# Decoder layer: key roundings moved between engines, the last cross values of a head put ahead, and the cross values of two key blocks made together

## The chip, the cores and the metric

One core of a Trainium2 chip runs the whole kernel. The metric is device time in microseconds (us), lower is better. Three timed executions of the kernel before took 523.75 to 525.77, median 524.22.

## The reference

A decoder layer on `x` (1024 queries, width 128, 16 heads of width 8), everything in fp32:

```
x = layernorm(x + self_attention(x))              # one shared key/value head, 1024 keys
x = layernorm(x + cross_attention(x, ctx, mask))  # 6404 keys, 16 heads, masked keys get -1e9
x = layernorm(x + expert(x))                      # router, top 1 of 8 experts, weight = its probability
```

`self_attention` and `cross_attention` are softmax(Q K^T / sqrt(8)) V with projections and biases. The mask kills a range of keys; with the data here two groups of 640 keys are live.

## The kernel before

**Layout.** Scores are computed twice. As *rows* (queries on partitions, keys along the free axis, into PSUM tiles `RT[0]`, `RT[1]`) they only give the maximum per query, which VectorE (DVE) reduces at L883. As *columns* (keys on partitions, 512 queries along the free axis, into `ST[0..2]`) with the maximum already subtracted they go through ScalarE's exponential (ACT, L1065) into `prob`, and TensorE (PE) multiplies `prob` by the values into `O` (L1199, the function `add_values`). A head's maxima are needed before its columns, so rows run one head ahead of the columns.

**Cross attention.** `T` counts a pair (640 keys, five blocks of 128) of a head. There are 16 heads and n = 2 pairs, 32 `T` in all. PE's order is written out by hand. `other_blocks` does blocks b = 1 to 4: the column product of query half 0 (k = 2b), a row product of unit b-1, the column product of half 1 (k = 2b+1), a row product, and then the values of block b-1. `next_blocks` does block 0 of the next `T`, row units 4 and 5 (short ones of 128 keys), and the values of block 4. `clear_o` zeroes `O` for a new head, once `copy_o` on ACT has emptied it. A column product and a row product use different halves of the array's rows (`STACK`) and run side by side; the values use 128 rows and four groups of 32 columns.

**What orders it.** Column product k writes bank `BANK[k]` and waits until the exponential that last used the bank is done: `AGAIN[k]` is how many products back that was.

```python
BANK = (2, 0, 1, 2, 0, 1, 0, 2, 0, 1)
AGAIN = tuple(min(d for d in range(1, NCOL) if BANK[k - d] == BANK[k]) for k in range(NCOL))
```

So products 6 and 8 have a distance of 2, 7 and 9 a distance of 4, the others 3. The values of block b wait for the exponentials of both of its halves. GpSimd (POOL) rounds the keys from `Kl` into `Kr` and `Kc`, copies values to `vst`, and splits the maxima; SyncE's (SP) queue loads keys and carries the maxima (`max_rows`).

**Between self and cross attention.** The last self head's sums (`den`) and outputs (`aTr`) come back by DMA, DVE takes the reciprocal (`sums_back`), PE spreads it and projects (`project_out`), the layernorm follows, PE transposes `x` and makes the first cross queries. The keys of the second pair are rounded by DVE (`keys_of_pair`). The same `project_out` follows cross attention, and then the router and the experts (L1516, L1523 on PE, L930 on DVE).

`warm_up(o, count)` is `count` throw-away products of 512 columns into a free bank.

Of the kernel before, what the change touches and what calls it, by code (L numbers as in the profile page):

```python
# [5 lines left out]
F32 = mybir.dt.float32  # L6
# [10 lines left out]
P = 128  # L17
# [24 lines left out]
RU = 6  # L42
# [17 lines left out]
def decoder_layer(nc, t, out):  # L60
    ctx = ExitStack()
    with ctx:
# [9 lines left out]
        def dram(name, shape, dt=F32):  # L72
# [117 lines left out]
            "in_xT in_w0 in_r in_w in_bo cst0 cst q_clean pen_rows bias_ready bias_moved parts_known "  # L190
            "w0_ready warm sel_made bq_scaled s_k_ready s_k_hi s_k_z s_k_stack s_v_ready bias_copied vs_made "
# [46 lines left out]
        def _(sp):  # L238
# [35 lines left out]
            def o_rows(a, g):  # L274
# [5 lines left out]
                load(den[g * DH:(g + 1) * DH, :], osb[DH:P:32, g % 2, :], a + "_o_back")  # L280
# [4 lines left out]
            def o_back(a):  # L285
# [5 lines left out]
                load(den[0:h * DH, :], od[a][0:h, :, DH, :], a + "_o_back")  # L291
# [119 lines left out]
        def _(pool):  # L411
# [40 lines left out]

            low_q("s")
# [39 lines left out]
            p0 = pool.snap(pool.value_load(steer[0:1, 0:1], min_val=0, max_val=NP - MIN_PAIRS))  # L493

# [117 lines left out]
        def _(dve):  # L612
# [71 lines left out]
            def stack_k(h):  # L684
                w = slice(h * HALF, (h + 1) * HALF)
                dve.wait_ge(S("s_k_hi"), h + 1)
                v.tensor_scalar(kz[:, w], ST[1 + h][:, :], rowk[:, 1:2], kcon[:, 0:1], ALU.mult, ALU.add) \
                    .then_inc(S("s_k_z"), 1)
                dve.wait_ge(S("s_k_z"), h + 1)
                v.scalar_tensor_tensor(out=Kself[:, w], in0=khi[:, w].bitcast(F32), scalar=rowk[:, 6:7], in1=kz[:, w],  # L690
                                       op0=ALU.mult, op1=ALU.add).then_inc(S("s_k_stack"), 1)

            stack_q0("s", 0)
            stack_k(0)
            dve.wait_ge(S("in_r"), 48)
            v.tensor_scalar(bq["s"][:, :], bq["s"][:, :], SCALE, None, ALU.mult).then_inc(S("bq_scaled"), 1)
# [25 lines left out]
            for r in range(HEADS * SELF_U):  # L722
# [6 lines left out]
                if r == 0:  # L729
                    stack_k(1)  # L730
                if r == 2:
                    stack_q0("s", 1)
# [52 lines left out]
            def keys_of_pair(c, i):  # L785

                dve.wait_ge(S("x_k_ready"), i + 1)
                if c and not isinstance(i, int):
                    dve.wait_ge(S("kd_out"), i * 64)
                v.tensor_scalar(kx_f[c][:, :], RT[1][:, 0:PAIR], bk_x[:, 0:1], None, ALU.add).then_inc(S("x_k_f"), 1)  # L790
                v.tensor_scalar(kx_hi[c][:, :], RT[1][:, 0:PAIR], bk_x[:, 0:1], None, ALU.add).then_inc(S("x_k_hi"), 1)
                dve.wait_ge(S("x_k_f"), i + 1)
                dve.wait_ge(S("x_k_hi"), i + 1)
                v.tensor_tensor(kx_lo[c][:, :], kx_f[c][:, :], kx_hi[c][:, :].bitcast(F32), ALU.subtract) \
                    .then_inc(S("x_k_lo"), 1)


            keys_of_pair(0, 0)
# [145 lines left out]
        def _(act):  # L944
# [69 lines left out]
            act.wait_ge(S("bq_scaled"), 1)  # L1014
# [25 lines left out]
            with act.Fori(0, n1) as i:  # L1040
                act.wait_ge(S("x_v_ready"), act.snap(i + 2))
# [539 lines left out]
```

## Time and profile before

| | |
|---|---|
| median of three timed executions | 524.22 us |
| the profiled execution | 524.29 us, its span 522.6 us |
| busy share of the span | PE 93%, DVE 82%, ACT 69%, POOL 37% |
| start to first self columns | 0 to 32.7 us |
| self attention | 32.7 to 203.4 us |
| between the attentions | 203.4 to 247.0 us |
| cross attention, first columns to last values | 247.0 to 472.8 us |
| project, router, experts, layernorm | 472.8 to 522.6 us |

The span is the time from the first to the last instruction of one profiled execution; 1.7 us lie outside it. A busy PE is not an array at its peak: products overlap and waits for the array's draining count as busy.

### The profile page before, as it was taken

The numbers are of one execution on the slowest core, as the hardware profiler recorded it, in microseconds if no ns is written. First come the engines' busy times: TensorE is split into PE (matmuls) and PEld (weight loads), VectorE is DVE, ScalarE is ACT, GpSimd is POOL, SyncE is SP. The second block draws the span as 40 slices with busy tenths as digits, with TensorE's granted clock in tenths as the row PEclk, the third lists the DMA queues.
The fourth block names the chain that finished last, engine by engine and source line by source line (L and its number), as shares of the span: only waits on it lengthen the run. The fifth ranks groups of instructions, "written<-read, shape, count | busy, mean of one in ns | idle before, by whom it ended". The sixth has DMA issues, their size and how long they took to land.

```text
span 522.6 us, 13768 instructions
## 1 busy us (share of the span) xinstructions
PE 486.1 (93%) x4122; PEld 199.5 (38%) x4122; DVE 430.0 (82%) x639; ACT 358.7 (69%) x682; POOL 192.3 (37%) x300
## 2 busy tenths in 40 slices
PE   7989999999999998578999999999999999998793
PEld 2423333333333344423344444444444444435441
DVE  4999999999999825759889899899999998704478
ACT  6238888888888864330778878788888888882220
POOL 3214889889890000032233333233333323210010
PEclk9999999999999999989899999999999999999698
DMA  3389997877300014423233111111111111011001
GB/s 93 100 261 325 278 327 284 306 285 291 144 13 12 12 54 132 149 62 99 48 69 79 40 38 38 40 32 34 38 36 32 35 36 32 25 56 44 1 0 43
DMA packets 21770, 52.56 MB, mean 101 GB/s; under 512 B 5021, under 2 KB 13375, under 8 KB 19649
## 3 DMA queue, kind: packets, MB, share of 16 engines
q1 hardware_dynamic: 18461, 22.46, 16.4%
q0 software_dynamic: 2304, 28.84, 14.7%
q8 instruction: 37, 0.61, 0.5%
q10 hardware_dynamic: 932, 0.37, 0.3%
q14 instruction: 36, 0.29, 0.2%
HBM read 42.10 MB, written 8.94 MB: 98 GB/s over the span
## 4 chain that ended last, share of the span: by engine, by line
PE 76%; DVE 12%; ACT 5%; issue 3%; DMA 2%; ACTq 0%; SPq 0%; DVEq 0%
PE O L1199 30%; PE ST L1425 14%; PE RT L1397 9%; PE ST L1230 9%; PE RT L1216 4%; DVE mxs L726 3%; ACT prob L1028 2%; DVE x L930 2%; PE RT L1523 2%; DMA Qs<-mxr 2%; DVE mxc L883 1%; ACT osb L989 1%; PE O L1170 1%; PE RT L1120 1%; PE O L1195 1%
## 5 line engine op out<-in xcount | busy, mean ns | idle before, releaser
L883 DVE TENSOR_REDUCE mxc<-RT 128x1024 f32 (+1 forms) x192 | 196.8, 1046 | 24.0 <-PE RT L1397 19.5
L1065 ACT ACTIVATE prob<-ST 128x512 f32<-128x512 f32 x320 | 175.2, 595 | 44.4 <-PE ST L1425 44.1
L1028 ACT ACTIVATE prob<-ST 128x512 f32<-128x512 f32 x256 | 138.6, 597 | 26.5 <-PE ST L1230 15.9
L726 DVE TENSOR_REDUCE mxs<-RT 128x2 f32<-128x1024 f32 x128 | 152.9, 1224 | 3.2 <-PE RT L1216 1.0
L1397 PE MATMUL RT<-Kr,Qs 64*128 64x128 f32 (+1 forms) x512 | 119.5, 373 | 3.7 <-ACT big L975 2.2
L1425 PE MATMUL ST<-Qs,Kc 64*128 64x512 f32 x320 | 121.3, 453 | 1.2 <-DMA Qs<-mxr 0.7
L1199 PE MATMUL O<-prob,vst 128*9 128x256 f32 x1280 | 99.7, 383 | 0.6 <-ACT prob L1065 0.6
L1216 PE MATMUL RT<-Kself,Qs 64*128 64x512 f32 x256 | 89.2, 450 | 3.2 <-DVE Kself L690 1.4
L1230 PE MATMUL ST<-Qs,Kself 64*128 64x512 f32 x256 | 91.2, 450 | 0.4 <-DMA Qs<-mxr 0.4
L1199 PE MATMUL O<-prob,Vs 128*9 128x256 f32 x1024 | 79.3, 381 | 1.5 <-ACT prob L1028 0.7
L1425 PEld LDWEIGHTS ST<-Qs,Kc 64*128 64x128 f32 x320 | 54.0, 186 | 52.5 <-ACT prob L1065 26.7
L1397 PEld LDWEIGHTS RT<-Kr,Qs 64*128 64x128 f32 x512 | 58.8, 185 | 31.0 <-DVE mxc L883 26.0
L509 POOL CAST Kr<-big 128x512 fp32r (+1 forms) x64 | 29.1, 456 | 94.0 <-DMA big<-pd 71.8
L465 POOL TENSOR_SCALAR big<-big 128x3520 uint8<-128x3520 uint32 x16 | 49.9, 3117 | 23.2 <-DMA big<-in_mask 23.1
L1230 PEld LDWEIGHTS ST<-Qs,Kself 64*128 64x128 f32 x256 | 37.4, 184 | 50.7 <-ACT prob L1028 37.5
L534 POOL COPY vst<-Vx 128x27 f32 x64 | 13.1, 205 | 106.7 <-PE O L1199 105.8
L1216 PEld LDWEIGHTS RT<-Kself,Qs 64*128 64x128 f32 x256 | 35.7, 184 | 11.5 <-DVE mxs L726 6.0
L1199 PEld LDWEIGHTS O<-prob,vst 128*9 128x9 f32 x1280 | 19.0, 88 | 51.3 <-ACT prob L1065 35.4
L509 POOL CAST Kc<-big 128x256 fp32r (+1 forms) x64 | 29.2, 456 | 24.9 <-PE ST L1425 24.7
L1199 PEld LDWEIGHTS O<-prob,Vs 128*9 128x9 f32 x1024 | 15.2, 88 | 45.1 <-ACT prob L1028 38.2
L469 POOL TENSOR_TENSOR big<-big 128x880 int32<-128x880 int32 x14 | 29.1, 2081 | 1.2
L949 ACT ACTIVATE rstd<-mv,eps 128x4 f32<-128x4 f32 x6 | 1.8, 297 | 27.5 <-DVE mv L815 27.5
(220 smaller groups left out, 349.2 us busy)
## 6 DMA issues: line engine op xcount, KB each, us to landing
big<-in_mask POOLq DMA_DIRECT2D x16, 1760.0 KB, 7.6
big<-kd SPq DMA_DIRECT2D x66, 80.0 KB
od_s<-osb SPq DMA_DIRECT2D x14, 128.0 KB, 3.1
od_x<-osb SPq DMA_DIRECT2D x14, 128.0 KB, 1.8
Qs<-qd_s SPq DMA_DIRECT2D x12, 128.0 KB, 6.9
Qs<-qd_x SPq DMA_DIRECT2D x12, 128.0 KB, 3.8
qd_s<-Vx SPq DMA_DIRECT2D x2, 512.0 KB, 4.0
qd_x<-big SPq DMA_DIRECT2D x2, 512.0 KB, 4.5
```

The lines of the kernel that those rows point to most:

```text
L465: g_.tensor_scalar(sums if q == 0 else dead8, maskI[m % 2].bitcast(U32), 1.0, 0.0, ALU.min, ALU.max) \
L469: g_.tensor_tensor(sums.bitcast(I32), sums.bitcast(I32), dead8.bitcast(I32), ALU.add) \
L509: g_.tensor_copy(dst, Kl[:, ds(slot, 1), k0:k1].rearrange("p o k -> p (o k)")).then_inc(S(name), 1)
L726: v.tensor_reduce(mxs[:, h % 2, c2, :].rearrange("p (f t) -> p f t", f=2)[:, :, q], RT[r % 2][:, :].rearrange("p (f k) -> p f k", f=2), AX ...
L883: v.tensor_reduce(o, src, AX.X, ALU.max).then_inc(S("x_row_free"), 1)
L1028: nc.scalar.activation(prob[:, c % SLOTS, k * HALF:(k + 1) * HALF], ST[(2 * c + k) % 3][:, :], ACT.Exp) \
L1065: nc.scalar.activation(prob[:, b, (k % 2) * HALF:(k % 2 + 1) * HALF], ST[BANK[k]][:, :], ACT.Exp) \
L1199: mm = mmul(O[32 * q:32 * q + VW, 0:256], v, prob[:, slot, q * 256:(q + 1) * 256], start=False, stop=False, skip_group_check=True)
L1216: mm = mmul(RT[r % 2][:, f * HALF:(f + 1) * HALF], Qs[STACK[f], h, q * P:(q + 1) * P], Kself[STACK[f], c2 * 512:(c2 + 1) * 512], start=Tru ...
L1230: mmul(ST[(2 * c + f) % 3][:, :], Kself[STACK[f], b * P:(b + 1) * P], Qs[STACK[f], g, :], start=True, stop=True).then_inc(S("s_col_ready"), 1)
L1397: mm = mmul(o, Qs[STACK[f], h, q * P:(q + 1) * P], Kr[STACK[f], w], start=True, stop=not gen, skip_group_check=True)
L1425: mm = mmul(o[:, :], Kc[STACK[f], b, :], Qs[STACK[f], g, :], start=True, stop=not gen, skip_group_check=True)
```

## The change

Key and query roundings at the start: the sign and sum of the second half of the self keys and of the second self head move from DVE (`stack_k(1)`, `stack_q0("s", 1)`) to POOL as two operations each, and the part `kz` of that half to ACT. The second pair's cross keys move from DVE to ACT (two roundings) and POOL (the difference). The wait for `den` is separated from the wait for `aTr`. In cross attention, `other_blocks` makes the values of blocks 0 and 1 together after block 2's scores and those of 2 and 3 together after block 4's; at a head change `next_blocks` makes row unit 4 and the last values ahead of the new head's column products. ACT copies `O` before the new head's first exponential. The first cross rows start before the other queries are projected. `warm_up` counts change from 16 to 14 and from 8 to 18 (after the output projection, in both attentions). The expert biases' eight products are split into two groups of four. `BANK` is unchanged.

```diff
-                load(den[g * DH:(g + 1) * DH, :], osb[DH:P:32, g % 2, :], a + "_o_back")
+                load(den[g * DH:(g + 1) * DH, :], osb[DH:P:32, g % 2, :], "den_in")
...
+            def stack(o, hi, z, sign, name):
+                g_.tensor_scalar(hi, hi.bitcast(F32), sign, None, ALU.mult).then_inc(S("stack_signed"), 1)
+                pool.wait_ge(S("stack_signed"), 1 if name == "s_k_stack" else 2)
+                g_.tensor_tensor(o, hi.bitcast(F32), z, ALU.add).then_inc(S(name), 1)
...
+            stack(Kself[:, HALF:Q], khi[:, HALF:Q], kz[:, HALF:Q], rowk[:, 6:7], "s_k_stack")
...
+            stack(Qs[:, 1, :], q0hi["s"][1], q0z["s"][1], rowk[:, 7:8], "s_q0_stack")
             low_q("s")
...
+            with pool.Fori(0, n1) as i:
+                wait_count(pool, S("x_k_f"), i + 2)
+                wait_count(pool, S("x_k_hi"), i + 2)
+                wait_count(pool, S("kd_out"), i * 64 + 64)
+                g_.tensor_tensor(kx_lo[1][:, :], kx_f[1][:, :], kx_hi[1][:, :].bitcast(F32), ALU.subtract) \
+                    .then_inc(S("x_k_lo"), 1)
...
-                if r == 0:
-                    stack_k(1)
-                if r == 2:
-                    stack_q0("s", 1)
...
             def sums_back(a):
-                dve.wait_ge(S(a + "_o_back"), 16 * 15)
+                dve.wait_ge(S("den_in"), 48 * ("sx".index(a) + 1))
                 v.reciprocal(rden[:, :], den[:, :]).then_inc(S(a + "_rden"), 1)
 
             def project_out(a):
+                dve.wait_ge(S(a + "_o_back"), 16 * 12)
...
-            dve.wait_ge(S("s_pv"), HEADS * SELF_U)
-            with dve.Fori(0, n1) as i:
-                keys_of_pair(1, dve.snap(i + 1))
...
+            nc.scalar.activation(kz[:, HALF:Q], ST[2][:, :], ACT.Identity, bias=kcon[:, 0:1], scale=rowk[:, 1:2]) \
+                .then_inc(S("s_k_z"), 1)
...
+                act.wait_ge(S("kd_out"), act.snap(i * 64 + 64))
+                nc.scalar.activation(kx_f[1][:, :], RT[1][:, 0:PAIR], ACT.Identity, bias=bk_x[:, 0:1]).then_inc(S("x_k_f"), 1)
+                nc.scalar.activation(kx_hi[1][:, :], RT[1][:, 0:PAIR], ACT.Identity, bias=bk_x[:, 0:1]).then_inc(S("x_k_hi"), 1)
...
             for g in range(HEADS):
                 T0 = act.snap(n * g)
-                step_exp(T0, 0)
                 if g:
                     copy_o("x", g - 1, act.snap(T0 * NBLK + NBLK))
+                step_exp(T0, 0)
                 step_exp(T0, 1)
...
-                    warm_up(ST[2], 16)
+                    warm_up(ST[2], 14)
...
-                warm_up(ST[2], 8)
+                warm_up(ST[2], 18)
...
-                        if turn:
+                        if b == 4 and h_turn is not None and h_turn < HEADS:
                             pe.wait_ge(S("x_mx_copied"), h_turn + 1)
-                        values(g, T, b - 1, e + 2 * b)
+
+                        if b % 2 == 0:
+                            values(g, T, b - 2, e + 2 * b)
+                            values(g, T, b - 1, e + 2 * b)
...
+                    if g != g_before and not first:
+
+                        if h < HEADS:
+                            rows(1, 4, h, U)
+                            rows(0, 4, h, U)
+                        values(g_before, T_before, NBLK - 1, e + NCOL)
+                        have_max("x", g)
+                        for f in range(2):
+                            col(g, T, f, e + (NCOL + 1 + f - AGAIN[f]))
+                            if h < HEADS:
+                                for q in (2, 3):
+                                    rows(1 - f, 5, h, U, [q])
+                        return
...
+                have_queries("x", 0)
+                if not gen:
+                    rows_alone(0, 0, range(2))
+                for h in range(2):
+                    project_q("x", wq_x, h, 1 + h)
+                rows_alone(0, 0, range(0 if gen else 2, RU))
+                with pe.Fori(1, n) as i:
+                    rows_alone(0, i, range(RU))
+                have_queries("x", 1)
+                rows_alone(1, n, range(1))
                 pe.wait_ge(S("x_q_high"), 2)
                 pe.wait_ge(S("x_q_full"), 2)
...
                 turn_max("x", 0, 1)
-                rows_alone(1, n, range(3, 4))
+                rows_alone(1, n, range(1, 4))
...
-                    if u == 5:
+                    if u in (5, 9):
 
                         pe.wait_ge(S("coefT_copied"), 2)
-                        for q in (4, 5, 6, 7, 0, 1, 2, 3):
+                        for q in range(4, 8) if u == 5 else range(4):
```

## Rows read from the trace of the kernel before

**Rows 1.** Windows: stretch, length; busy PE, PEld, DVE, ACT, POOL; clock; DMA.

```profile
247.00:457.00 210.00, 208.17 (x1989) 89.68 (x1989) 186.91 (x192) 167.88 (x325) 68.69 (x205) 0.99 0.17 42
492.00:522.60 30.60, 20.85 (x58) 9.40 (x58) 23.87 (x100) 4.36 (x8) 2.54 (x2) 0.83 0.06 18
```

**Rows 2.** Timeline, PE, first pair of a cross head (start, us, what).

```profile
391.06 0.50 PE L1425 MATMUL ST<-Qs,Kc 64*128 64x512 f32 x1
...
392.41 0.50 PE L1425 MATMUL ST<-Qs,Kc 64*128 64x512 f32 x1
...
392.75 0.39 PE L1425 MATMUL ST<-Qs,Kc 64*128 64x512 f32 x1
393.08 0.62 PE L1199 MATMUL O<-prob,vst 128*9 128x256 f32 x8
393.67 0.50 PE L1425 MATMUL ST<-Qs,Kc 64*128 64x512 f32 x1
...
394.97 0.50 PE L1425 MATMUL ST<-Qs,Kc 64*128 64x512 f32 x1
...
396.23 0.50 PE L1425 MATMUL ST<-Qs,Kc 64*128 64x512 f32 x1
...
397.71 0.45 PE L1425 MATMUL ST<-Qs,Kc 64*128 64x512 f32 x1
```

**Rows 3.** Timeline, PE, second pair of that head: values, maxima turned, head change.

```profile
399.79 0.62 PE L1199 MATMUL O<-prob,vst 128*9 128x256 f32 x8
400.23 0.38 PE L1170 MATMUL O<-ident,mxh 128*16 128x128 f32 x2
...
403.10 0.50 PE L1425 MATMUL ST<-Qs,Kc 64*128 64x512 f32 x1
...
405.13 0.49 PE L1425 MATMUL ST<-Qs,Kc 64*128 64x512 f32 x1
```

**Rows 4.** Groups of instructions: the throw-away products of `warm_up` into ST.

```profile
L1120 PE MATMUL ST<-wrow 128*128 128x512 bf16 x32 | 7.4, 379 | 0.0
```

**Rows 5.** Timeline, ACT, the first exponentials of that first pair.

```profile
391.68 1.09 ACT L1065 ACTIVATE prob<-ST 128x512 f32<-128x512 f32 x2 [0.44 <-PE ST L1425]
```

**Rows 6.** Timeline, PE, the last blocks of the last head (no rows left).

```profile
469.24 0.50 PE L1425 MATMUL ST<-Qs,Kc 64*128 64x512 f32 x2
...
470.50 0.50 PE L1425 MATMUL ST<-Qs,Kc 64*128 64x512 f32 x2 [0.17 <-ACT prob L1065]
...
472.25 0.62 PE L1199 MATMUL O<-prob,vst 128*9 128x256 f32 x8 [0.64 <-ACT prob L1065]
```

**Rows 7.** Windows, the whole head of Rows 2 and 3.

```profile
391.06:405.13 14.07, 13.95 (x136) 5.97 (x136) 12.79 (x14) 11.36 (x23) 4.70 (x15) 1.00 0.14 40
```

**Rows 8.** Timeline, DVE, at the start and between the attentions.

```profile
16.32 2.35 DVE L726 TENSOR_REDUCE mxs<-RT 128x2 f32<-128x1024 f32 x2
...
207.81 0.95 DVE L836 RECIPROCAL rden<-den 128x128 f32<-128x128 f32 x1 [1.89 <-DMA aTr<-osb]
208.68 0.79 DVE L790 TENSOR_SCALAR prob<-RT,bk_x 128x640 f32<-128x640 f32 x1
...
211.73 1.28 DVE L842 TENSOR_TENSOR prob<-aTr,RT 128x512 f32<-128x512 f32 x2
```

**Rows 9.** Timeline, PE, the first cross row products.

```profile
229.31 0.50 PE L1397 MATMUL RT<-Kr,Qs 64*128 64x512 f32 x2 [2.20 <-ACT big L975]
```

**Rows 10.** Windows with a lowered clock, between the attentions and at the end.

```profile
221.40:224.80 3.40, 3.03 (x8) 0.87 (x8) 0.00 (x0) 1.18 (x3) 0.85 (x2) 0.50 0.20 50
...
487.60:492.00 4.40, 3.72 (x20) 3.34 (x17) 0.00 (x0) 0.59 (x1) 0.00 (x0) 0.51 0.01 4
492.00:498.00 6.00, 6.00 (x9) 2.70 (x10) 4.15 (x18) 0.26 (x1) 0.00 (x0) 0.51 0.00 0
```

**Rows 11.** Timeline, DVE, the reciprocal after cross attention.

```profile
476.84 0.95 DVE L836 RECIPROCAL rden<-den 128x128 f32<-128x128 f32 x1 [2.30 <-DMA aTr<-osb]
```

**Rows 12.** Groups of instructions: the experts' sums on DVE.

```profile
L930 DVE SCALAR_TENSOR_TENSOR x<-RT,lg,x 128x128 f32<-128x128 f32 x64 | 17.1, 344 | 3.9 <-PE RT L1523 3.8
```

More of the change, by code:

```diff
@@ L189, in decoder_layer @@
         sems = {n_: sem(n_) for n_ in (
-            "in_xT in_w0 in_r in_w in_bo cst0 cst q_clean pen_rows bias_ready bias_moved parts_known "
-            "w0_ready warm sel_made bq_scaled s_k_ready s_k_hi s_k_z s_k_stack s_v_ready bias_copied vs_made "
+            "in_xT in_w0 in_r in_w in_bo cst0 cst stack_signed q_clean pen_rows bias_ready bias_moved parts_known "
+            "w0_ready warm sel_made den_in s_k_ready s_k_hi s_k_z s_k_stack s_v_ready bias_copied vs_made "
             "mask_in0 mask_in1 mask_used mask_added mask_counts counted flags flag_sums steered pen_made "
@@ L290, in o_back @@
                     load(aTr[0:h * DH, q * 256:(q + 1) * 256], od[a][0:h, q, 0:DH, :], a + "_o_back")
-                load(den[0:h * DH, :], od[a][0:h, :, DH, :], a + "_o_back")
+                load(den[0:h * DH, :], od[a][0:h, :, DH, :], "den_in")
             def more_queries(a, h):
@@ L451, in load_mask @@
                     .then_inc(S(f"mask_in{m % 2}"), 16)
+            def stack(o, hi, z, sign, name):
+                g_.tensor_scalar(hi, hi.bitcast(F32), sign, None, ALU.mult).then_inc(S("stack_signed"), 1)
+                pool.wait_ge(S("stack_signed"), 1 if name == "s_k_stack" else 2)
+                g_.tensor_tensor(o, hi.bitcast(F32), z, ALU.add).then_inc(S(name), 1)
+            pool.wait_ge(S("s_k_z"), 1)
+            pool.wait_ge(S("s_k_hi"), 2)
+            pool.wait_ge(S("s_k_stack"), 1)
+            stack(Kself[:, HALF:Q], khi[:, HALF:Q], kz[:, HALF:Q], rowk[:, 6:7], "s_k_stack")
+            pool.wait_ge(S("s_q0_hi"), 2)
+            pool.wait_ge(S("s_q0_z"), 2)
+            pool.wait_ge(S("s_q0_stack"), 1)
+            stack(Qs[:, 1, :], q0hi["s"][1], q0z["s"][1], rowk[:, 7:8], "s_q0_stack")
             low_q("s")
@@ L682, in stack_q0 @@
                                        op0=ALU.mult, op1=ALU.add).then_inc(S(a + "_q0_stack"), 1)
[L684 to L691, printed above, removed]
             stack_q0("s", 0)
-            stack_k(0)
+            dve.wait_ge(S("s_k_hi"), 1)
+            ch(v.tensor_scalar(kz[:, 0:HALF], ST[1][:, :], rowk[:, 1:2], kcon[:, 0:1], ALU.mult, ALU.add))
+            v.scalar_tensor_tensor(out=Kself[:, 0:HALF], in0=khi[:, 0:HALF].bitcast(F32), scalar=rowk[:, 6:7],
+                                   in1=kz[:, 0:HALF], op0=ALU.mult, op1=ALU.add).then_inc(S("s_k_stack"), 1)
             dve.wait_ge(S("in_r"), 48)
-            v.tensor_scalar(bq["s"][:, :], bq["s"][:, :], SCALE, None, ALU.mult).then_inc(S("bq_scaled"), 1)
+            v.tensor_scalar(bq["s"][:, :], bq["s"][:, :], SCALE, None, ALU.mult).then_inc(S("bias_moved"), 1)
             def split_max(h, reduced):
@@ L783, in _, with keys_of_pair @@
             n = dve.snap(n1 + 1)
[L785 to L794, printed above, removed]
+            def keys_of_pair():
+                dve.wait_ge(S("x_k_ready"), 1)
+                v.tensor_scalar(kx_f[0][:, :], RT[1][:, 0:PAIR], bk_x[:, 0:1], None, ALU.add).then_inc(S("x_k_f"), 1)
+                v.tensor_scalar(kx_hi[0][:, :], RT[1][:, 0:PAIR], bk_x[:, 0:1], None, ALU.add).then_inc(S("x_k_hi"), 1)
+                dve.wait_ge(S("x_k_f"), 1)
+                dve.wait_ge(S("x_k_hi"), 1)
+                v.tensor_tensor(kx_lo[0][:, :], kx_f[0][:, :], kx_hi[0][:, :].bitcast(F32), ALU.subtract) \
                     .then_inc(S("x_k_lo"), 1)
-            keys_of_pair(0, 0)
+            keys_of_pair()
             dve.wait_ge(S("vx_ones"), 1)
@@ L1051, in _ @@
             act.wait_ge(S("w0_ready"), 2)
-            act.wait_ge(S("bias_moved"), 2)
+            act.wait_ge(S("bias_moved"), 3)
             act.wait_ge(S("kd_out"), n * 64)
@@ L1372, in _ @@
                 project_q0("x", h)
-            for h in range(2):
-                project_q("x", wq_x, h, 1 + h)
             def cross(gen):
@@ L1484, in rows_alone @@
                             rows_pairwise(h, U)
-                        warm_up(O, 2 if u < 4 else 1)
+                        warm_up(ST[0], 2 if u < 4 else 1)
+                have_queries("x", 0)
[8 more added lines that the diff above has]
+                rows_alone(1, n, range(1))
                 pe.wait_ge(S("x_q_high"), 2)
                 pe.wait_ge(S("x_q_full"), 2)
-                pe.wait_ge(S("x_q0_z"), DIRECT)
-                have_queries("x", 0)
-                with pe.Fori(0, n) as i:
-                    rows_alone(0, i, range(RU))
-                have_queries("x", 1)
-                rows_alone(1, n, range(3))
                 turn_max("x", 0, 1)
-                rows_alone(1, n, range(3, 4))
+                rows_alone(1, n, range(1, 4))
                 for g in range(HEADS):
```

3 lines of the change are left out of this document (2 added, 1 removed).

## The prediction

> **What bounds the kernel.** I read the stretches first. Cross attention is the longest part that the change touches: PE is busy 208 of 210 us, DVE 187, ACT 168 [rows 1]. One head alone says the same: of 14.07 us PE is busy 13.95, DVE 12.79, ACT 11.36 [rows 7]. PE's busy time counts draining and weights, so I went to its timeline. The starts of the column products of blocks 1 to 4, of the next block 0 and of the next block 1 are 391.06, 392.41, 393.67, 394.97, 396.23 and 397.71 [rows 2]: blocks of 1.26 to 1.35, then 1.48, together 6.65 for the pair. A block of 1.26 is 0.34 from the first to the second product, 0.33 to the values, 0.59 to the next block. The second pair with the head change takes 7.42, from 397.71 [rows 2] to 405.13 [rows 3].
>
> Two things stand behind these 1.26, and they are nearly equal, which decides this change. One is PE's own work. The other is the way through ACT: from a column product's start 0.62 passes to its exponential (391.06 to 391.68), and two exponentials, which overlap, take 1.09 [rows 2, 5], one alone about 0.6. So a bank is free 0.62 + 0.60 + 0.04 = 1.26 after the product that wrote it began, and the values can follow 0.62 + 1.09 + 0.04 = 1.75 after the first product of their block. Both are seen bare where no rows are left: 469.24 to 470.50 is 1.26, released by ACT, and 470.50 to 472.25 is 1.75, released by ACT [rows 6].
>
> **The change, part by part.**
>
> *What pairing the values saves.* Followed by work of the same shape (the turned maxima, 16 columns wide) a values group takes 399.79 to 400.23, 0.44 [rows 3]; followed by scores it takes 0.55 to 0.59 (393.08 to 393.67) [rows 2]. Throw-away products of 512 columns follow each other every 0.23 (7.4 us over 32) [rows 4], and score products in one run should too, against 0.34 and 0.33 after and before values [rows 2]. So one change of shape there and back costs about 0.12 + 0.11 + 0.11 = 0.34. A pair of 640 keys had five values groups standing alone and now has three runs of them; two are saved, 64 in all, 21.8 us of PE time.
>
> *What it costs.* The column products 2, 3, 4, 5 now come in a run with three banks, then the values of blocks 0 and 1, both behind the exponential of product 3. Before, a values group lay between each wait and its cause. I follow one pair from product 2's start:
> - values 0 start 1.75 later (ACT; PE itself could at about 1.6, since product 5 waits for product 2's bank until 1.26);
> - values 0 and 1 to product 6: 0.44 + 0.55 = 1.0;
> - product 8 shares product 6's bank: 1.26;
> - product 8 to values 2: 0.67 (392.41 to 393.08) [rows 2];
> - values 2 and 3 to the next product 0: 1.0;
> - from there as before to the next product 2: 1.48.
>
> Sum 7.16, against 6.65: 0.51 more. The saved 0.68 is there, and 1.2 of waiting stands against it. POOL's roundings and copies keep their order and were not late; behind the waiting column product queue the row products, so DVE gets them later, but it has 1.3 us of slack in a head [rows 7].
>
> The second pair: 2.75, 0.15 for the turned maxima (now in front of product 6, after values, of one shape with them), 2.93, then the head change. There the row products of unit 4 and the values go first (0.35), 0.55 to product 0, 0.28 to product 1 and 0.6 for clearing `O` behind ACT's copy: 1.8, where before it was 2.03 (403.10 to 405.13) [rows 3]. Sum 7.64 against 7.42, 0.22 more. With the copy ahead of the new head's first exponential, its second starts late and pushes product 3's in the next pair by 0.13. Per head 0.51 + 0.13 + 0.22 = 0.86; 14 heads with rows, 12.0 us. In the last four pairs rows are partly or wholly missing, and the waits for ACT weigh more: 0.64 + 1.4 + 0.66 + 0.43 = 3.1, by the same steps. Cross attention: +15.2. An error of 0.2 in a pair is 6 us, so I keep +9 to +19.
>
> The Trainium skill (TensorEngine Tiling, Key Properties) says that a change of tiling mode drains the engine. The trace agrees, 0.44 against 0.55 to 0.59. By that rule alone, with nothing else late, the sum of this part would be minus 21.8, the first rival below. The skill also says (TensorE: Matmul & The Clock Gate, Part 3) that products stay in program order and only weight loads are pulled ahead. That speaks against the change, for nothing passes a waiting product; the bare 1.26 and 1.75 agree.
>
> *Between the attentions.* DVE's reciprocal waited 1.89 for the last `aTr`; `den` is issued before these and I take it 0.8 earlier, of which PE can use 0.4. Then DVE rounded keys, three operations of 0.8 to 0.9 from 208.68, and only at 211.73 made `aT` [rows 8], while PE had spread the reciprocal. ACT and POOL do this now, beside idle time; their difference on POOL I bound by 0.83 (as DVE) and 2.5. `aT` comes 2.0 earlier in all. The clock fell to half (1.2 GHz) from 221.4 to 224.8 after PE had stood idle [rows 10], and the first cross queries were made there; with 18 throw-away products the idle time shrinks, 0.9 saved. The first cross rows waited 2.20 for ACT's last query rounding [rows 9], which they no longer need. 2.0 + 0.9 + 2.2 = 5.1 at the first rows. The later queries' projections now stand between units 1 and 2 and let DVE wait 0.6, so 4.5 at the first columns. Bounds 2 (SP's key loads set the rows' start) and 5.5.
>
> *At the end.* The reciprocal waited 2.30 for `aTr` [rows 11]: I take 1.3 of it, bounds 0 and 2.3. The products of 14 instead of 16 are hidden in that. From 487.6 to 498 the clock was at half [rows 10]: the router and the first experts. At 2.4 GHz throughout, router and first experts come 1.7 and 1.2 earlier, and DVE's 17.1 us of sums lose half of their 3.9 of waiting [rows 12]: 4.8. But PE still has little to do from the layernorm through the router's short products, so the clock may fall anyway, later and for less long; I take 3.2 of the 4.8. The biases in two groups cover part of that waiting and are counted there. Sum 4.5, bounds 1.3 and 7. DVE, busy 23.87 of 30.60 here [rows 1], stays.
>
> *At the start.* Three operations of about 0.75 leave DVE, but PE's other products (1.4 a unit) set rows 2 to 6, so its maxima, 2.35 for two [rows 8], come only 0.3 earlier; bounds 0 and 2.2. POOL's two-step versions are unknown in length: from 1.3 to 2.6 each, needed two units later, hidden.
>
> **Sum.** 524.3 (the profiled run; its span 522.6 and 1.7 outside; the median of the runs is 524.22) + 15.2 - 4.5 - 4.5 - 0.3 = 530.2.
>
> **Rivals.** Forecast, 530, chance 0.50: within its own bounds 525 to 535, and 0.07 of it lies below 0.5%.
>
> *The draining sets the pace (faster).* If the exponentials are in time behind the runs, PE saves up to 21.8, but DVE's 12.79 in a head of 14.07 [rows 7] allows 1.3 a head, about 19: 524.3 - 19 - 9.3 = 496. It speaks for it that PE is busy 99% there; against it, the bare 1.75 and 1.26. It decides if the way from product to values is 0.25 shorter at both waits of a pair. Chance 0.12.
>
> *The waits give half back.* Weights are loaded and the array is drained while PE waits, so that runs after a wait start sooner than my rows say; 0.25 in a pair, cross +7: 522. For it: my steps carry 0.1 of draining after each wait. Chance 0.20, 0.12 of it within 0.5%.
>
> *The ends don't deliver.* The clock falls in both places and SP's loads hold the first rows: 524.3 + 15.2 - 2 - 2.5 - 0.3 = 535. For it: the short transposes did not hold the clock before. Chance 0.18.
>
> A difference of about 0.5%, 2.6 us, is what a measurement of this kernel can tell from none. Slower by more: 0.43 + 0.18 = 0.61. Within: 0.07 + 0.12 = 0.19. Faster: 0.08 + 0.12 = 0.20. The range leaves out the first rival and the outermost of the others: 516 to 536; the forecast's own is 525 to 535.
>
> **What the changed profile would show.** First pair of a head near 7.2 and head near 14.9 (near 12.8: first rival); values pairs released by ACT 1.75 after product 2 and 6; product 8 1.26 after product 6; 0.44 between the two values groups of a run. First columns near 242.5, the first row products near 224.3. The clock at full through the first cross queries, and a shorter half-clock stretch at the router. `rden` about 1.3 earlier after the last values. I am wrong if ACT is no releaser of the values, or if PE's wait at product 8 is missing.

## The result, and the profile after

Four executions of the changed kernel took 531.36 to 535.16 us, median 532.79; four of the kernel before, beside them, 523.75 to 526.70, median 525.00. The ratio is 1.015, 95% interval 1.010 to 1.020: slower, where 530.2 and a range of 516 to 536 stood. The profiled execution is the longest of the four, 535.16, its span 533.5. It is 10.9 above the profiled one of before, the medians 7.8. Medians and ratios here are of fast executions alone; the sixth execution of project_first, below, took 522.15 at a mean clock of 0.967 and is left out.

The table takes starts from the timelines: of the first self columns, of the last values group of self attention, of the first cross row products and columns, of the last values group of cross attention.

| us | before | after |
|---|---|---|
| start to first self columns | 32.70 | 32.86 |
| to the last self values | 170.74 | 173.33 |
| from there to `rden` | 4.37 | 3.35 |
| ... to the first cross rows | 25.87 | 21.06 |
| ... to the first columns | 43.60 | 42.19 |
| first columns to last values | 225.21 | 238.12 |
| of these up to product 2 of the second head | 16.91 | 16.57 |
| ... the next 13 heads, from product 2 to product 2 | 183.55 | 194.66 |
| ... from there to the last values (four pairs) | 24.75 | 26.89 |
| last values to the end | 50.35 | 47.00 |

(Heads are counted from product 2, since the new order puts product 0 about 1.1 later in the head change.) So cross attention gives 12.9 away, the stretch between the attentions brings 1.4, the end 3.4. The 2.6 in self attention are the profiled execution's own: PE waits there 2.9 for `Qs<-mxr`, 0.4 in the profile before, and in the other profiles of this study self attention took 171.3 with the old start and 170.3 to 171.8 with the new one. It would account for the 2.4 by which the profiled execution lies above its median.

One stretch of half clock of the kernel before lies inside cross attention, in its first head, from 248.7 to 252.1; the changed kernel has none there. A window out of it:

```profile
249.00:251.00 2.00, 2.00 (x13) 0.51 (x14) 1.17 (x2) 0.94 (x2) 0.40 (x1) 0.50 0.60 88
```

So 12.9 is the loss of the new loop less what that stretch had cost. The run ends_only, below, tells the two apart.

From the pages, the same two groups (busy, mean ns | idle before, what ended it), the kernel before and then the changed one:

```profile
L883 DVE TENSOR_REDUCE mxc<-RT 128x1024 f32 (+1 forms) x192 | 196.8, 1046 | 24.0 <-PE RT L1397 19.5
L1425 PE MATMUL ST<-Qs,Kc 64*128 64x512 f32 x320 | 121.3, 453 | 1.2 <-DMA Qs<-mxr 0.7
...
L891 DVE TENSOR_REDUCE mxc<-RT 128x1024 f32 (+1 forms) x192 | 197.4, 1047 | 37.4 <-PE RT L1410 32.0
L1438 PE MATMUL ST<-Qs,Kc 64*128 64x512 f32 x320 | 120.8, 453 | 18.1 <-ACT prob L1080 18.0
```

PE now stands idle 18.1 us in front of column products, where it was 1.2, and ACT's exponential ends 18.0 of it. DVE, which could have gained, waits more. The windows that answer to [rows 1] and [rows 7]: 210 us of cross attention and one head.

```profile
248.40:458.40 210.00, 194.31 (x1894) 94.44 (x1894) 180.05 (x183) 156.06 (x307) 65.19 (x197) 1.00 0.16 40
...
398.80:413.78 14.98, 13.92 (x140) 6.72 (x136) 12.81 (x14) 11.17 (x22) 4.72 (x15) 1.00 0.12 34
```

A head takes 14.98 where [rows 7] had 14.07, and the busy time of PE, DVE and ACT in it is the same to within 0.2. No engine has more work; PE has 1.0 of idle time more. Where it stands is in the timeline, the first pair of that head and the start of the second, answering to [rows 2]:

```profile
399.41 3.05 ACT L1080 ACTIVATE prob<-ST 128x512 f32<-128x512 f32 x6
...
399.72 0.50 PE L1438 MATMUL ST<-Qs,Kc 64*128 64x512 f32 x1
...
401.53 1.05 PE L1214 MATMUL O<-prob,vst 128*9 128x256 f32 x16
402.51 0.49 PE L1438 MATMUL ST<-Qs,Kc 64*128 64x512 f32 x1
402.52 0.72 PE L1410 MATMUL RT<-Kr,Qs 64*128 64x512 f32 x2
402.85 0.39 PE L1438 MATMUL ST<-Qs,Kc 64*128 64x512 f32 x1
...
403.77 0.49 PE L1438 MATMUL ST<-Qs,Kc 64*128 64x512 f32 x1 [0.53 <-ACT prob L1080]
...
404.52 1.05 PE L1214 MATMUL O<-prob,vst 128*9 128x256 f32 x16
405.50 0.50 PE L1438 MATMUL ST<-Qs,Kc 64*128 64x512 f32 x1
...
406.98 0.45 PE L1438 MATMUL ST<-Qs,Kc 64*128 64x512 f32 x1
```

Product 2 starts at 399.72, the two values groups (x16) 1.81 later, product 6 0.98 after them. Product 8 follows product 6 by 1.26, its wait released by ACT; the values 0.75 after it; product 0 0.98 later; the next product 2 1.48 later. Sum 7.26, where [rows 2] has 6.65. That the values wait at 401.53 shows only in the starts, since PE's last product still counts as busy. ACT's row says why it is 1.81 and not 1.75: six exponentials without a gap from 399.41 on, behind the copy of `O`. The exponential of product 3 ends at 401.48, 0.05 before the values start, and that of product 6 at 403.72, 0.05 before product 8 starts; over the heads the medians of both steps are 0.05 too.

Between the attentions, DVE and PE (answering to [rows 8, 9]):

```profile
209.54 0.95 DVE L846 RECIPROCAL rden<-den 128x128 f32<-128x128 f32 x1 [0.87 <-DMA den<-osb]
...
211.93 0.69 DVE L853 TENSOR_TENSOR prob<-aTr,RT 128x512 f32<-128x512 f32 x1 [0.65 <-PE RT L1358]
...
234.09 2.36 DVE L891 TENSOR_REDUCE mxc<-RT 128x1024 f32 x2 [2.97 <-PE RT L1410]
```

```profile
227.25 0.80 PE L1410 MATMUL RT<-Kr,Qs 64*128 64x512 f32 x2 [3.73 <-POOL Kr L531]
...
228.94 0.79 PE L1410 MATMUL RT<-Kr,Qs 64*128 64x512 f32 x2
...
230.50 3.02 PE L1155 MATMUL ST<-xT,wq_x 128*128 128x512 f32 x4
233.44 0.50 PE L1410 MATMUL RT<-Kr,Qs 64*128 64x512 f32 x2
```

The first rows now wait for POOL's key rounding, not for ACT. POOL in turn had waited for the load of the keys:

```profile
226.54 0.84 POOL L531 CAST Kr<-big 128x512 fp32r<-128x512 f32 x2 [12.17 <-DMA big<-pd]
```

The queries were rounded by 226.22, so the load was the last to come, by 0.3. Then come the projections, 3.02 long, and DVE waits 2.97 for unit 2. The stretches of lowered clock, answering to [rows 10]:

```profile
225.95:232.75 6.80, 5.50 (x11) 2.22 (x12) 2.72 (x3) 0.30 (x1) 0.84 (x2) 0.50 0.18 50
502.43:509.25 6.82, 6.82 (x14) 3.68 (x14) 3.99 (x17) 0.26 (x1) 0.00 (x0) 0.50 0.00 0
```

Half clock (1.2 GHz) still comes in both places: counted from the last self values 1.8 later between the attentions, and longer there (6.8 against 3.4), over the rows and the projections; it began 2.4 into the 3.73 that PE stood idle in front of the rows. At the router it is 6.8 long where it was 10.2. The reciprocal at the end, answering to [rows 11], and the experts' sums, to [rows 12]:

```profile
489.28 0.95 DVE L846 RECIPROCAL rden<-den 128x128 f32<-128x128 f32 x1 [0.48 <-DMA den<-osb]
```

```profile
L938 DVE SCALAR_TENSOR_TENSOR x<-RT,lg,x 128x128 f32<-128x128 f32 x64 | 17.1, 343 | 3.4 <-PE RT L1557 3.4
```

It starts 2.77 after the last values instead of 4.59; the sums wait 3.4 instead of 3.9.

### The profile page after: what moved, and what is told of

It reads as the page before. It is cut to its first block, busy times and chain, and to the rows that moved or that the text cites. A ratio compares the mean times of both kernels' runs of the same rounds, so it can differ in the third digit from the quotient of the medians.

```text
span 533.5 us, 13797 instructions
## 1 busy us (share of the span) xinstructions
PE 485.3 (91%) x4133; PEld 211.5 (40%) x4140; DVE 426.6 (80%) x633; ACT 357.4 (67%) x685; POOL 198.4 (37%) x305
## 4 chain that ended last, share of the span: by engine, by line
PE 72%; DVE 7%; ACT 7%; DMA 6%; issue 4%; SPq 1%; ACTq 1%; POOL 0%; DVEq 0%; POOLq 0%
PE O L1214 26%; PE ST L1438 14%; PE RT L1410 9%; PE ST L1245 8%; DMA Qs<-mxr 4%; PE RT L1231 4%; ACT prob L1080 4%; PE RT L1557 3%; ACT prob L1038 2%; DVE mxs L742 2%; DVE mxc L891 2%; PE ST L1135 1%; PE RT L1135 1%; PE O L1185 1%; DVE x L938 1%
## 5 line engine op out<-in xcount | busy, mean ns | idle before, releaser
L1080 ACT ACTIVATE prob<-ST 128x512 f32<-128x512 f32 x320 | 168.6, 602 | 41.3 <-PE ST L1438 39.8
L1038 ACT ACTIVATE prob<-ST 128x512 f32<-128x512 f32 x256 | 138.6, 597 | 29.1 <-PE ST L1245 18.8
L1438 PE MATMUL ST<-Qs,Kc 64*128 64x512 f32 x320 | 120.8, 453 | 18.1 <-ACT prob L1080 18.0
L1410 PE MATMUL RT<-Kr,Qs 64*128 64x128 f32 (+1 forms) x512 | 124.0, 381 | 5.6 <-POOL Kr L531 3.7
L1214 PE MATMUL O<-prob,vst 128*9 128x256 f32 x1280 | 87.1, 380 | 0.4 <-ACT prob L1080 0.4
L1438 PEld LDWEIGHTS ST<-Qs,Kc 64*128 64x128 f32 x320 | 55.3, 184 | 70.0 <-ACT prob L1080 51.8
L1410 PEld LDWEIGHTS RT<-Kr,Qs 64*128 64x128 f32 x512 | 64.1, 185 | 31.9 <-issue 15.5
L1214 PEld LDWEIGHTS O<-prob,vst 128*9 128x9 f32 x1280 | 25.7, 89 | 38.5 <-ACT prob L1080 22.1
L1214 PEld LDWEIGHTS O<-prob,Vs 128*9 128x9 f32 x1024 | 15.2, 88 | 45.1 <-ACT prob L1038 37.4
L997 ACT COPY osb<-O 128x256 f32<-128x256 f32 x32 | 11.9, 373 | 20.7 <-PE O L1214 20.7
```

The costliest lines, as they stand in the source:

```text
L1038: nc.scalar.activation(prob[:, c % SLOTS, k * HALF:(k + 1) * HALF], ST[(2 * c + k) % 3][:, :], ACT.Exp) \
L1080: nc.scalar.activation(prob[:, b, (k % 2) * HALF:(k % 2 + 1) * HALF], ST[BANK[k]][:, :], ACT.Exp) \
L1214: mm = mmul(O[32 * q:32 * q + VW, 0:256], v, prob[:, slot, q * 256:(q + 1) * 256], start=False, stop=False, skip_group_check=True)
L1410: mm = mmul(o, Qs[STACK[f], h, q * P:(q + 1) * P], Kr[STACK[f], w], start=True, stop=not gen, skip_group_check=True)
L1438: mm = mmul(o[:, :], Kc[STACK[f], b, :], Qs[STACK[f], g, :], start=True, stop=not gen, skip_group_check=True)
```

## Experiments

Theory P is the prediction's: the paired values wait behind the exponentials, and that costs more than the saved draining. Its rivals are named in each expectation. All medians stand against the kernel before on the same chip. (Where an expectation gives the length of the end, it counts from about 0.2 later than the tables here.)

### Which part costs: four kernels

**pair_only** is the kernel before with this alone:

```diff
-                        if turn:
+                        if b == 4 and h_turn is not None and h_turn < HEADS:
                             pe.wait_ge(S("x_mx_copied"), h_turn + 1)
-                        values(g, T, b - 1, e + 2 * b)
+                        if b % 2 == 0:
+                            values(g, T, b - 2, e + 2 * b)
+                            values(g, T, b - 1, e + 2 * b)
```

> The kernel before with only the values of blocks 0 and 1, and of 2 and 3, made together. Theory P (waiting behind the exponentials costs more than the saved draining): the first pair of a head is 7.25 as in the changed kernel, the second about 7.9 (7.72 there, and about 0.2 that the old head change takes more), a head 15.1 instead of 14.07, in all 524.3 + 15 = 539. Rival D (draining sets the pace, and the head change's new order is what costs): a head of 13.4 or less, in all 514 or less.

**head_order** is the kernel before with the other part of the cross loop alone, the new branch of `next_blocks` and

```diff
-                step_exp(T0, 0)
                 if g:
                     copy_o("x", g - 1, act.snap(T0 * NBLK + NBLK))
+                step_exp(T0, 0)
```

> The kernel before with only the new order at a head change (row unit 4 and the last values first) and ACT's copy of O ahead of the new head's first exponential. Theory P: the second pair of a head loses 0.23 in the change of head and gets about 0.1 back from the late second exponential, 15 heads, 524.3 - 2 = 522. Rival D: this is what costs, a head near 15, about 537.

**single_values** is the changed kernel with the first diff reversed:

> The changed kernel with only the pairing of the values undone: each values group behind its own block's two products again. Theory P: heads of 13.95, the ends' gain of 4.7 (1.4 between the attentions, 3.3 at the end) stays, 524.3 - 4.7 - 2 = 518. Rival D: no faster than the changed kernel, 532 or more.

**ends_only** is the changed kernel with both reversed:

> The changed kernel with the whole cross loop of the kernel before (single values, old head change, old place of the copy). Theory P: heads of 14.07, 524.3 - 4.7 = 519.6; against single_values it prices the head change at 1 to 2. Rival E (the new places of the roundings and of the query projections cost as much elsewhere as they save): 524.

| us | median | ratio, 95% interval | to first columns | cross | 13 heads | end |
|---|---|---|---|---|---|---|
| pair_only | 543.02 | 1.033 (1.027 to 1.040) | 43.57 | 243.53 | 196.39 | 49.81 |
| head_order | 523.21 | 0.997 (0.993 to 1.002) | 43.57 | 224.22 | 182.29 | 49.02 |
| single_values | 515.67 | 0.981 (0.974 to 0.989) | 41.18 | 222.32 | 181.69 | 45.36 |
| ends_only | 516.12 | 0.983 (0.977 to 0.990) | 41.38 | 222.97 | 182.72 | 45.34 |

The pairing is the whole loss. Alone it costs 18 us, and undoing it alone turns a kernel 1.5% slower into one 1.9% faster: 17 us between the two. Rival D is out. In heads with rows the pairs of pair_only take 7.20 and 7.90 (median over the heads), as expected; head_order's take 6.68 and 7.29 where 6.65 and 7.41 were, 0.09 a head where 0.13 was expected. In time neither head_order against before nor single_values against ends_only can be told from none. The two kernels with single values also have a faster end than the changed kernel by 1.6. Their code there is the same, and half clock at the router lasted 3.4 in their profiles and 6.8 in its; why it differs from execution to execution no run shows, so these 1.6 are not the pairing's.

ends_only has the cross loop of the kernel before, with the changed surroundings, and no half clock in its first head. It takes 222.97 where the kernel before takes 225.21: 1.3 of these 2.2 lie before product 2 of the second head, the rest in single longer heads. Against it the changed loop costs 238.12 - 222.97 = 15.2. The stretch in the first head stands in all three profiles with the old stage between the attentions (before, pair_only, head_order) and in none of the other eleven; what in that stage removes it was not tested.

pair_only lost more in its last four pairs than theory P had: 29.4 from product 2 of the 15th head to the last values against 24.8 before and 26.9 in the changed kernel. Its clock was at half from 478.4 to 485.3 there, in the last head, which no other kernel shows, and the pair under it took 9.05 where the changed kernel's took 6.62.

The page of single_values has the wait gone (the line of the changed kernel has 18.1):

```profile
L1438 PE MATMUL ST<-Qs,Kc 64*128 64x512 f32 x320 | 120.6, 453 | 0.7 <-ACT prob L1080 0.7
```

### Which wait: other banks

**banks** is the changed kernel with

```diff
-BANK = (2, 0, 1, 2, 0, 1, 0, 2, 0, 1)
+BANK = (0, 1, 2, 0, 1, 2, 1, 0, 2, 1)
```

> The changed kernel with other banks, so that the products with a distance of 2 are 1 and 6 and no longer 6 and 8: product 8 no longer waits for the exponential of 6. Theory P: the values of blocks 2 and 3 then wait for the exponential of product 7 itself, 1.75 after product 6 where it is 1.26 + 0.67 = 1.93 now, so a pair gains about 0.18, in all 5.8: 532.8 - 5.8 = 527. Rival B (the wait at product 8 is the whole loss): 0.6 a pair, 514.

523.76, ratio 0.998 (0.995 to 1.001), 9.0 under the changed kernel. (The profiled execution took 528.88: its clock was at half from 14.6 to 31.7, before self attention. That does not touch the cross loop.) Of the 9.0 1.6 are the end, whose stretch of half clock was 3.4 long here. Cross attention takes 230.23 instead of 238.12, 7.9 less where 5.8 was expected; a pair 7.00 and 7.47 instead of 7.25 and 7.72, 0.25 each. PE's timeline of a pair:

```profile
400.66 0.50 PE L1438 MATMUL ST<-Qs,Kc 64*128 64x512 f32 x1
401.00 0.63 PE L1438 MATMUL ST<-Qs,Kc 64*128 64x512 f32 x2
401.92 0.50 PE L1438 MATMUL ST<-Qs,Kc 64*128 64x512 f32 x1
402.41 1.05 PE L1214 MATMUL O<-prob,vst 128*9 128x256 f32 x16
```

Product 6 at 400.66, its values at 402.41: 1.75 exactly, where it was 2.01. So the wait at product 8 is 0.26 of the loss in a pair, and when it is gone the wait for the exponential of product 7 stands right behind: it ends at 402.36. (The row at 401.00 holds products 7 and 8: 8 starts at 401.24.) Rival B is out: the values of blocks 2 and 3 need the exponential of product 7 as well, and so start 1.75 after product 6, the first of its run.

### What pairing would save if nothing had to be waited for

Two pairs of kernels with work left out. In **pace_single** and **pace_paired**:

```diff
-                nc.scalar.activation(prob[:, b, (k % 2) * HALF:(k % 2 + 1) * HALF], ST[BANK[k]][:, :], ACT.Exp) \
+                nc.scalar.activation(prob[:, b, (k % 2) * HALF:(k % 2) * HALF + 128], ST[BANK[k]][:, 0:128], ACT.Exp) \
...
-                        src = RT[u % 2][:, :].rearrange("p (f k) -> p f k", f=2)
+                        src = RT[u % 2][:, :].rearrange("p (f k) -> p f k", f=2)[:, :, 0:256]
```

> single_values with work left out, to take ACT and DVE off PE's path: each cross exponential does 128 of its 512 columns and the maxima of the long row units look at 256 of 512 keys. PE's instructions are the same. Theory P (a change of shape there and back costs PE 0.34, and only the waits hid that): PE alone sets a head, somewhat under 13.98; this run is the partner of pace_paired.

> The changed kernel with the same work left out. Theory P: with no waits left the pairing saves 0.68 a pair against pace_single, 1.36 a head, about 20 in all. Rival N (the draining that pairing saves is small, and the pairing costs by itself): within 5 of pace_single, or above it.

504.45 and 511.56: the paired kernel is still the slower one by 7. Theory P's 20 less did not come. The sign is rival N's, but not yet its reason. Pairs took 6.38 and 7.08 single, 6.52 and 7.41 paired, and PE's timeline of pace_paired still has a wait at product 8 in it, since even a short exponential's result comes 0.94 after the product's start:

```profile
400.89 0.50 PE L1438 MATMUL ST<-Qs,Kc 64*128 64x512 f32 x1
...
401.83 0.50 PE L1438 MATMUL ST<-Qs,Kc 64*128 64x512 f32 x1 [0.21 <-ACT prob L1080]
```

So this comparison was not free of waits. **pace2_single** and **pace2_paired** take the maxima down to 64 and 32 keys too, and have the `BANK` of the run banks.

> Like pace_single, with all maxima cut further (64 keys of a long unit, 32 of each short tile) and the banks of the run banks, so that nothing but PE is left in a pair. Theory: a head a little under the 13.46 of pace_single, about 13.3; it is the partner of pace2_paired.

> The changed kernel cut in the same way. In pace_paired ACT still held product 8 (0.27) and DVE's maximum a row product (about 0.2). Theory S (only the way out of the values costs PE something, 0.11 a run, as their 0.98 for two against twice 0.55 shows): 0.22 a pair under pace2_single, 7 in all. Theory D (0.34 for a change there and back, as the prediction had it): 0.68 a pair, 20 in all. Rival N (nothing is saved): equal.

499.03 and 497.18, which the intervals (0.949 to 0.955, 0.946 to 0.956) can't tell apart. Cross attention took 207.96 and 204.45, a head (median) 13.23 and 12.90, the first pair 6.39 and 6.19. With rows, pairing saves 0.17 a pair (0.20 and 0.14); in the last four pairs it loses 1.4 (21.20 and 22.58). That is theory S's number and not D's 20, but the timelines say that the comparison wasn't free of waits either. Two blocks of pace2_single first:

```profile
404.25 0.50 PE L1438 MATMUL ST<-Qs,Kc 64*128 64x512 f32 x1
...
404.91 0.62 PE L1214 MATMUL O<-prob,vst 128*9 128x256 f32 x8
405.46 0.49 PE L1438 MATMUL ST<-Qs,Kc 64*128 64x512 f32 x1
...
406.12 0.62 PE L1214 MATMUL O<-prob,vst 128*9 128x256 f32 x8
406.67 0.49 PE L1438 MATMUL ST<-Qs,Kc 64*128 64x512 f32 x1
```

and of pace2_paired:

```profile
403.46 0.49 PE L1438 MATMUL ST<-Qs,Kc 64*128 64x512 f32 x1
...
403.80 0.62 PE L1438 MATMUL ST<-Qs,Kc 64*128 64x512 f32 x2
...
404.03 0.39 PE L1410 MATMUL RT<-Kr,Qs 64*128 64x512 f32 x1
404.40 0.49 PE L1438 MATMUL ST<-Qs,Kc 64*128 64x512 f32 x1
...
404.83 1.05 PE L1214 MATMUL O<-prob,vst 128*9 128x256 f32 x16
405.81 0.50 PE L1438 MATMUL ST<-Qs,Kc 64*128 64x512 f32 x1
```

Two blocks take 2.42 single (1.21 each) and 2.35 paired. The row at 403.80 holds two column products, and the second starts at 404.03, with the row product beside it. So the four products of the run start at 403.46, 403.80, 404.03 and 404.40, and the values at 404.83: steps of 0.34, 0.23, 0.37 and 0.43. The 0.23 is what the prediction took for score products in one run. The 0.37 is a wait. Product 5 uses the bank of product 2, whose exponential, short as it is, ends at 404.35:

```profile
404.07 0.28 ACT L1080 ACTIVATE prob<-ST 128x128 f32<-128x128 f32 x1 [1.21 <-PE ST L1438]
```

Product 5 starts 0.05 after that, and so does product 9 after the exponential of product 6 (medians over the heads); the profile lists no wait, because PE's last product still counts as busy. What a change of shape costs can be read from three steps in these two timelines: the second product of a run comes 0.34 after the first and the third 0.23 after the second; the last product of a block is followed by values after 0.32 (404.59 to 404.91), where it would be 0.23 to another product; and two values groups in a run take 0.98, against twice 0.55. That is about 0.1 each time, about 0.3 for a change there and back, near the prediction's 0.34. By these steps a run of four without the wait would reach its values 0.34 + 0.23 + 0.23 + 0.32 = 1.12 after it began, not 1.37. That is an estimate: 0.25 a run, 0.5 a pair, on top of the 0.17 that was measured. What pairing saves with nothing to wait for was therefore not measured; it would take a fourth bank, or exponentials that are left out.

### The ends: who holds the clock

**counts** is single_values with `warm_up` at 16 and 8 again.

> single_values with the throw-away products' old counts, 16 and 8. The runs so far show stretches of half clock of 3.4, 6.8 and 10.2 at the router, and 3.4 more of it make the end about 1.65 longer (45.1, 46.8). Theory C (the 18 products hold the clock): 10.2 at the router as before, the end 3.3 longer, 48.4, and between the attentions up to 1 later; in all 519. Rival: the counts do nothing, 515.7.

**project_first** is single_values with

```diff
-                have_queries("x", 0)
-                if not gen:
-                    rows_alone(0, 0, range(2))
                 for h in range(2):
                     project_q("x", wq_x, h, 1 + h)
-                rows_alone(0, 0, range(0 if gen else 2, RU))
+                have_queries("x", 0)
+                rows_alone(0, 0, range(RU))
```

> single_values with the projections of the other cross queries back ahead of the first rows, still without the wait for their rounding. In single_values PE stands idle about 3.5 for POOL's first key rounding, the clock falls, and units 2 on wait for the projections at half clock (3 between the maxima of units 1 and 2). Theory G (that gap takes the projections for nothing): first columns 2 to 3 earlier after the last self values, 515.7 - 2.5 = 513.2. Rival: the columns hang on SP's later key loads, no gain, 515.7.

**first_warm** adds one line to it, ahead of `turn_max("x", 0, 1)`: `warm_up(ST[0], 4)`.

> project_first with four throw-away products ahead of the turning of the first cross maxima, where PE stands idle for about 0.9. In project_first the clock fell there, from 240.1 to 243.5, and the rows of units 1 to 3 took 1.69 a unit in place of 1.13. If the products hold it: first columns 1.7 earlier, 513.4 - 1.7 = 511.7. If the clock falls all the same: 513.4.

| us | median | ratio, 95% interval | to first rows | to first columns | half clock between | end | half clock at the router |
|---|---|---|---|---|---|---|---|
| counts | 517.38 | 0.986 (0.983 to 0.989) | 23.90 | 45.45 | 206.2 to 209.6, 219.8 to 233.5 | 47.34 | 6.8 |
| single_values | 515.67 | 0.981 (0.974 to 0.989) | 21.03 | 41.18 | 226.1 to 229.5 | 45.36 | 3.4 |
| project_first | 512.85 | 0.974 (0.969 to 0.979) | 22.15 | 40.56 | 205.9 to 209.3, 240.1 to 243.5 | 47.00 | 6.8 |
| first_warm | 512.09 | 0.975 (0.973 to 0.978) | 21.06 | 38.81 | none | 45.32 | 3.4 |

(All four have cross attention at 222.2 to 222.3. Rows and columns count from the last self values.) The windows of lowered clock in counts, project_first and first_warm, in this order:

```profile
219.80:233.50 13.70, 11.22 (x24) 3.79 (x24) 3.96 (x4) 4.64 (x8) 0.85 (x2) 0.50 0.22 58
486.00:492.90 6.90, 6.78 (x20) 4.93 (x21) 2.22 (x10) 0.32 (x2) 0.00 (x0) 0.51 0.00 0
```

```profile
240.10:243.50 3.40, 3.40 (x10) 0.83 (x8) 2.45 (x2) 0.00 (x0) 0.00 (x0) 0.50 0.58 139
```

```profile
481.90:485.30 3.40, 3.40 (x6) 1.51 (x6) 2.21 (x10) 0.26 (x1) 0.00 (x0) 0.50 0.00 0
```

With the old counts the clock falls at the first transposes and stays at half over first queries, rows and projections: 4.3 later at the first columns in this execution. Part of it may be the early stretch (206.2 to 209.6), which only counts and project_first have; but project_first, with 18 products behind the same early stretch, kept full clock over the transposes and queries. Over all executions the mean granted clock is 0.972 to 0.980 in counts and 0.982 to 0.990 in single_values, so that the old counts lose clock is shown. How much time it costs is not: the medians are 1.7 apart, and the interval of counts lies inside that of single_values. At the end theory C had 10.2 of half clock at the router and got 6.8. The end is 2.0 longer, but five profiles with the new counts have 6.8 there as well, so this can't be put down to the counts.

In project_first the projections went into PE's idle time and units 1 and 2 came 0.97 apart. From first rows to first columns it takes 18.4 instead of 20.2, a gain of 1.7; but this execution has the early stretch of half clock too, which put its rows 1.1 later, so 0.6 is left of it. And the clock now fell later, at 240.1, where PE had waited for the first maxima. With four throw-away products there it did not fall: 17.8 from rows to columns, 0.7 less. (One profiled execution of each; that the products did it is likely, not shown.) The first columns then wait for the next thing, as PE's timeline of first_warm shows:

```profile
243.19 0.50 PE L1438 MATMUL ST<-Qs,Kc 64*128 64x512 f32 x2 [0.26 <-DMA Qs<-mxr]
```

That they come 1.75 earlier than in project_first, as the expectation had it, is therefore by 1.1 the luck of the early stretch. Over the whole kernel first_warm (512.09) and project_first (512.85) can't be told apart, nor first_warm and single_values by the intervals. It is the fastest median of this study among kernels that leave nothing out, 2.5% under the kernel before.

Across all profiles the end is 45.3 to 45.4 long where half clock lasted 3.4 (five kernels) and 47.0 to 47.3 where it lasted 6.8, with the changed kernel's end; with the old one it is 49.0 at 6.8 and 49.8 to 50.4 at 10.2.

## Why the prediction was right, and where its terms were off

**The cross loop, +15.2: right in mechanism, measured +12.9.** The heads with rows are the number that the prediction rested on: 0.86 a head. Over the 13 heads after the first it is 194.66 - 183.55 = 11.1, 0.85 a head. Its pair of 7.16 took 7.25, the second, 7.64, took 7.72. The values start 1.81 after product 2 and product 8 1.26 after product 6, ACT is the releaser, and two values groups take 0.98. (The sign "1.75 after product 2 and 6" contradicts its own steps, which give 1.26 + 0.67 = 1.93 after product 6; it was 2.01.) The two waits of `other_blocks` are shown by banks: taking one away gives 0.25 a pair and uncovers the next. Of the 2.3 that are missing to 15.2, the first head has 1.2: up to product 2 of the second head it is 0.3 less where 0.9 more was forecast, since the half clock from 248.7 to 252.1 is gone, a term that the prediction did not have. The last four pairs have 1.0: they took 2.1 more, not 3.1. Against ends_only, without that half clock, the loop costs 15.2; that it is the forecast to the tenth is in part luck, since single terms were off by nearly 1.

**The saved draining, 21.8: not measured, and its price per change holds.** The steps in pace2_paired show 0.23 for score products in a run and about 0.1 at each of three changes, as the prediction had it. That pairing saved only 0.17 a pair there is no proof against it, for the last product of each run was still waiting. The first rival had 0.12. The same wait speaks against it more plainly than the prediction did: with three banks and four products in a run, the last one waits for the exponential of the first, 0.94 after that one began even with exponentials of 128 columns, where PE alone would be there after 0.34 + 0.23 + 0.23 = 0.80 (an estimate from the steps above). The second rival, waits that give 0.25 a pair back, is out: the pairs took 0.09 and 0.08 more than the steps, not less. Of the Trainium skill's rule (TensorEngine Tiling, Key Properties), that a change of mode drains the engine, the runs show about 0.1 in each of three steps: from the first to the second product behind values, from the last product to the values, and from the values to the next product.

**Between the attentions, -4.5: measured -1.4.** Up to the first rows 5.1 was foreseen and 4.8 measured (25.87 to 21.06), with 2.0 for `aT`, which came 2.5 earlier. The number held, but what sets it is the key load, which the prediction had as a bound (2) and the last rival as its reason; queries and keys were ready within 0.3 of each other, so that this came out is luck in part. The step that failed is "let DVE wait 0.6": it waited 3.0. The clock was at full over the first queries, as foreseen, but it then fell in the idle time in front of the rows, and rows and projections ran at half, for 6.8 where the queries had had 3.4. The projections took 3.02 there, against 1.98 at full clock in first_warm. first_warm shows that the rest of the sum was there: with the projections in the idle time and the clock held the first columns come 4.8 earlier than before.

**The end, -4.5: measured -3.4.** `rden` came 1.8 earlier, not 1.3. Of the clock's 3.2 about 1.3 came: 10.2 of half clock became 6.8, and head_order, with the old end, has 49.02 at 6.8 against 50.35 at 10.2. The remaining 2.0 are `rden` and the biases. In single_values and four other profiles half clock at the router was 3.4 and the end 45.3 to 45.4, so the term is 3.4 or 5.0 by the execution.

**The start, -0.3: measured about -0.4.** From the first self rows (13.14 before, 13.69 after) to the first columns it is 19.56 and 19.17. The first rows start between 12.8 and 13.8 in the profiles of this study, with either start. POOL's two steps took 1.57 and 1.27, so each two-step version took 2.9, above its upper bound of 2.6, and was hidden all the same.

**Sum.** Forecast +5.9, measured +7.8 in medians and +10.9 in the profiled executions: 0.2 + 2.6 - 1.4 + 12.9 - 3.4. A forecast 2.3 too high in the cross loop and one too hopeful in the two ends (by 3.1 and 1.1) partly cancelled, which is luck. The last rival, that the ends don't deliver, was half true: they brought 4.8 of 9, and both of its reasons were at work, the clock and the key loads.

## What to carry to other kernels

Before grouping like work to save switches, follow one item from its cause to its consumer: if the producer's way is as long as one step of the loop, as here with 1.26 against 1.26, the switch was hiding a wait, and grouping uncovers it. Price a switch from single steps (first to second product after it, second to third), and before you believe a comparison without waits, see whether a product starts 0.05 after the end of what frees its bank: here the profile listed no wait, and 0.25 a run was still one. And where throw-away products hold the clock, it can fall in the next idle stretch, as it did here in front of the first rows: see where PE stands idle next, and put real work that is already due there first.

## What had not been expected of the hardware

Column and row products of 512 columns, side by side on the two halves of the array's rows, follow each other after 0.34 just behind values and after 0.23 within a run (pace2_paired), the same as the throw-away bf16 products over 128 rows with 0.22 to 0.23. Lowered clock came in stretches of 3.4, 6.8, 10.2, 13.7 and 17.1 us in these traces, and at the router 3.4 more of it went with an end about 1.65 longer.
